# A linear-attention and expert kernel: the batch laid anew, with k projected early into another bank and v one batch ahead

## The reference, cut

```python
mod = (silu(c) @ wmod).reshape(16, 6, 1, 128)            # sa, ca, ga, sb, cb, gb for each batch
h = layernorm(x) * (1 + ca) + sa                         # x: 16 batches x 512 tokens x 128
# attention, 16 heads of 8, 32 random features:
q = (exp(qh @ orf.T / 8**0.25 - |qh|^2 / (2*sqrt(8))) + 1e-6) / sqrt(32)     # k the same way
kv = einsum('nlm,nld->nmd', k, v);  ksum = k.sum(1)
out = (q @ kv) / (q @ ksum)
x = x + ga * (out @ Wo.T + bo)
h = layernorm(x) * (1 + cb) + sb
e = argmax(h @ gate_W + gate_b)                          # one of 8 experts for each token
x = x + gb * (gelu(h @ W1[e] + b1[e]) @ W2[e] + b2[e])
```

## Time and profile before

| what | us |
|---|---|
| median of 3 runs | 383.06 |
| lowest and highest | 382.57, 385.99 |
| span of the profiled execution, first to last instruction | 360.6 |
| first phase in it, up to about | 212 |
| TensorE busy in the span | 338.8 (94%) |
| VectorE, ScalarE, GpSimd busy | 271.2, 265.1, 213.2 |

### The profile page before, as it was taken

How to read it: one execution, slowest core, us unless ns; L and a number is a source line. 1 busy time by engine, 2 the same in 40 slices (tenths; PEclk the granted TensorE clock), 3 DMA queues, 4 the chain that set the end, 5 groups by cost and what they waited for, 6 DMA issues and landing times.

```text
span 360.6 us, 13729 instructions
## 1 busy us (share of the span) xinstructions
PE 338.8 (94%) x4823; PEld 263.9 (73%) x4823; DVE 271.2 (75%) x1104; ACT 265.1 (74%) x644; POOL 213.2 (59%) x262
## 2 busy tenths in 40 slices
PE   6899999899988999998999999999999999999994
PEld 5445765566465566646665669999989999999993
DVE  3456997898879789878887978887677676666653
ACT  2688988799878888977888756676656667666761
POOL 3142386776667757857854618846767455545554
PEclk9999999999999999999999999999999999999999
DMA  7174656774566547444432467445657665545410
GB/s 233 50 253 166 210 184 221 259 243 160 177 227 205 176 167 230 163 132 156 153 133 100 149 163 227 142 118 150 194 161 269 209 184 147 147 128 135 137 38 12
DMA packets 40211, 60.47 MB, mean 168 GB/s; under 512 B 5426, under 2 KB 28086, under 8 KB 40016
## 3 DMA queue, kind: packets, MB, share of 16 engines
q1 hardware_dynamic: 33776, 42.54, 39.9%
q0 software_dynamic: 6368, 17.05, 12.5%
HBM read 28.63 MB, written 19.34 MB: 133 GB/s over the span
## 4 chain that ended last, share of the span: by engine, by line
PE 60%; ACT 15%; DMA 10%; DVE 6%; issue 5%; POOL 1%; SPq 1%; DVEq 1%; POOLq 0%; ACTq 0%
PE ps_proj L1350 16%; PE ps_feat L1337 9%; DMA qmix<-qsqs 9%; PE ps_proj L1132 6%; PE ps_den_gate L1337 4%; PE ps_proj L1182 4%; PE ps_kv L1337 4%; ACT qf L627 3%; ACT qvals L606 2%; ACT shared L588 2%; PE ps_kv L1198 2%; PE ps_out L1330 2%; ACT den L656 2%; ACT shared L581 2%; ACT kvm L600 2%
## 5 line engine op out<-in xcount | busy, mean ns | idle before, releaser
L545 POOL DMA_INDIRECT out<-kf,modb x71 | 70.1, 987 | 52.4 <-DVE kf L1060 47.0
L507 POOL DMA_INDIRECT experts_lists<-pay,slot x64 | 65.9, 1030 | 43.4 <-DVE slot L893 29.5
L1350 PE MATMUL ps_proj<-w2sb,qf 128*128 x568 | 75.0, 275 | 0.4 <-ACT qf L690 0.4
L1350 PEld LDWEIGHTS ps_proj<-w2sb,qf 128*128 128x128 f32 x568 | 68.9, 192 | 0.6 <-issue 0.6
L681 ACT ACTIVATE xT<-ps_out 128x128 f32<-128x128 f32 x71 | 19.7, 277 | 44.8 <-PE ps_out L1330 44.1
L1055 DVE TENSOR_TENSOR kf<-ps_proj,firsts_sb 128x128 f32<-128x128 f32 x71 | 20.7, 291 | 34.6 <-PE ps_proj L1350 22.6
L690 ACT ACTIVATE qf<-ps_feat,shared 128x128 f32<-128x128 f32 x144 | 40.9, 374 | 0.0
L1337 PE MATMUL ps_feat<-xT,shared 128*128 128x128 f32 x288 | 38.8, 277 | 1.5 <-issue 0.9
L1337 PEld LDWEIGHTS ps_feat<-xT,shared 128*128 128x128 f32 x288 | 35.0, 192 | 2.8 <-issue 1.7
L1132 PE MATMUL ps_proj<-shared,wsb 128*128 128x512 f32 x62 | 33.3, 620 | 1.0 <-ACT shared L581 0.4
L977 DVE COPY shared<-firsts_sb 128x516 f32 x71 | 31.4, 442 | 1.6 <-issue 1.5
(11 more groups left out here) (189 smaller groups left out, 890.3 us busy)
## 6 DMA issues: line engine op xcount, KB each, us to landing
modb<-experts_lists SPq DMA_DIRECT2D x71, 196.0 KB, 2.8
xall<-in_x SPq DMA_DIRECT2D x16, 256.0 KB, 3.0
pay<-modb SPq DMA_DIRECT2D x16, 256.0 KB, 3.0
qmix<-qvals SPq DMA_DIRECT2D x30, 128.0 KB
qmix<-qsqs SPq DMA_DIRECT2D x30, 128.0 KB
modb<-modulation_rows SPq DMA_DIRECT2D x4, 768.0 KB, 5.2
firsts_sb<-in_firsts SPq DMA_DIRECT2D x8, 322.0 KB, 4.2
w2sb<-in_w SPq DMA_DIRECT2D x8, 256.0 KB
```

Of the source, the lines that this page charges most:

```text
L507: g_.indirect_dma_start(out=lists, in_=pay[b.home][:, t, :], in_offset=None, out_offset=bass.IndirectOffsetOnAxis(ap=slot[b.home][:, t:t + ...
L545: g_.indirect_dma_start(out=rows_out, in_=yb[u], in_offset=None, out_offset=bass.IndirectOffsetOnAxis(ap=token, axis=0), bounds_check=last ...
L1350: ins = mm(Y[u % 2][:, 0:D], g[u % R4][:, c * P:(c + 1) * P], w2sb[:, bass.ds(e * DFF + c * D, D)], start=(c == 0), stop=(c == FC - 1))
```

## The change

No matmul, activation or DMA is added or removed; they are reordered, and three semaphores replace one.

- On TensorE `transpose_xn(b+1)` and the k projection of b+1 go right behind `k_features(b)` and `transpose_h2(b-2)`. The k projection writes G (`k_bank`), once `attention(b-1)` has read it. `q_features(b)` follows, then `out_project(b-1)`, the v projection of b+1 (before: that of b, ahead of the output product), `gate(b-2)`, `kv_product(b)`, the q projection of b+1, `kv_transpose(b)`, `gate_transpose(b-2)`, the constants and the denominator, `rank(b-2)`, the numerator.
- On ScalarE `modulate(b+1)` stands between the two `k_pair`s, `k_values` and `k_squares` of b+1 ahead of `q_pair(b, 0)`, `gateT` between the `q_pair`s; v's values, q's values and q's squares of b+1 follow `kvm_copy(b)`, ahead of `Ln` and `Exp`.
- On VectorE `centre_h2(b-1)` goes ahead of `kv_values(b)`; its half of `normalise1(b+2)` stands behind that; `experts(b-2)`, `eps_values`, `scale_h2` and then `slots(b-2)` follow.
- On GpSimd the first layer norm's roots go ahead of the second's.
- The first and the last batch have orders of their own.

The helpers' waits follow the new semaphores (`s_pk`, `s_pq`, `s_pv` for `s_proj`); that part, and the first batch's q features as a function of their own, are left out here.

```diff
@@ -335,6 +337,9 @@
         block = ctx.enter_context(nc.Block())
+        def k_bank(v):
+            return PJ[0] if v < 2 else G
+
...
@@ -469,6 +474,8 @@
                 if b is not None:
                     pool.wait_ge(s_xn1, b.v)
+                    if b.v > 2:
+                        pool.wait_ge(s_xna, b.v - 2)
...
@@ -514,10 +523,10 @@
                     pool.wait_ge(s_mb, 16)
                 if b.v >= EARLY_ROWS and (b.v - EARLY_ROWS) % LATE_ROWS == 0:
                     pool.wait_ge(s_mbl, 16 * ((b.v - EARLY_ROWS) // LATE_ROWS + 1))
+                if ahead and b.par == 0:
+                    rstd1_of(b.half + 3, b=b + 2)
                 if not first:
                     rstd2_of(b + -1, rows_of=None if second else b + -2)
-                if ahead and b.par == 0:
-                    rstd1_of(b.half + 3, b=b + 2)
                 if not first and not second:
                     scatter(b + -2, (0, 1))
...
@@ -634,30 +643,60 @@
                 act.wait_ge(s_lg, b.v + 1)
                 a.activation(lgT[:], I[:, 0:P], ACT.Copy).then_inc(s_lgT, 1)
-            def batch(b, first=False, second=False, last=False, ahead=True):
-                k_pair(b, 0)
-                if not first and not second:
-                    h2T_copy(b + -2)
-                k_pair(b, 1)
-                if not first and not second:
-                    gateT(b + -2)
-                v_values(b)
-                q_pair(b, 0, first)
-                if not last:
-                    modulate(b + 1)
-                q_pair(b, 1, first)
-                kvm_copy(b)
-                if not last:
-                    k_values(b + 1)
-                    k_squares(b + 1)
-                    q_values(b + 1)
+            def rden_first(b):
                 act.wait_ge(s_den, b.v + 1)
                 act.wait_ge(s_eps, b.v + 1)
                 a.activation(den[:], G[:], ACT.Ln, bias=kveps[:, 1:2]).then_inc(s_denp, 1)
                 act.wait_ge(s_denp, b.v + 1)
                 a.activation(rden[:], den[:], ACT.Exp, scale=-1.0).then_inc(s_rden, 1)
-                if not last:
-                    q_squares(b + 1)
+
+            def first_batch(b):
+                k_pair(b, 0)
+                k_pair(b, 1)
+                v_values(b)
+                q_pair(b, 0, first=True)
+                modulate(b + 1)
+                q_pair(b, 1, first=True)
+                k_values(b + 1)
+                k_squares(b + 1)
+                kvm_copy(b)
+                v_values(b + 1)
+                q_values(b + 1)
+                q_squares(b + 1)
+                rden_first(b)
+                normalise1(b + 2)
+
+            def last_batch(b):
+                k_pair(b, 0)
+                h2T_copy(b + -2)
+                k_pair(b, 1)
+                gateT(b + -2)
+                q_pair(b, 0)
+                q_pair(b, 1)
+                kvm_copy(b)
+                rden_first(b)
+
+            def batch(b, first=False, second=False, last=False, ahead=True):
+                if first:
+                    return first_batch(b)
+                if last:
+                    return last_batch(b)
+                k_pair(b, 0)
+                modulate(b + 1)
+                k_pair(b, 1)
+                if not second:
+                    h2T_copy(b + -2)
+                k_values(b + 1)
+                k_squares(b + 1)
+                q_pair(b, 0)
+                if not second:
+                    gateT(b + -2)
+                q_pair(b, 1)
+                kvm_copy(b)
+                v_values(b + 1)
+                q_values(b + 1)
+                q_squares(b + 1)
+                rden_first(b)
                 if b.v + 2 < B:
                     normalise1(b + 2)
...
@@ -729,6 +768,7 @@
             def centre_h2(b):
+                dve.wait_ge(s_var2, b.v + 1)
...
                                                  scalar=mv2[:, t, 0:1], in1=modb[:, b.v, CB, :],
@@ -776,8 +816,6 @@
                 dve.wait_ge(s_shift1, b.v + 1 if b.v < 2 else b.half + 2)
                 if b.v:
                     dve.wait_ge(s_t1, b.v)
-                if b.v >= 2:
-                    dve.wait_ge(s_xna, b.v - 1)
...
@@ -994,32 +1032,32 @@
                         first_moments(b.half + 2, marked=x_stats(b + 3, 1))
                     else:
                         x_stats(b + 3, 0)
-                if not first and not last:
-                    normalise1(b + 1, lo=LT // 2)
                 if not first:
                     residual(b + -1)
                     second_stats(b + -1)
+                if second:
+                    dve.wait_ge(s_mb, 16)
+                if b.v > EARLY_ROWS and (b.v - 1 - EARLY_ROWS) % LATE_ROWS == 0:
+                    dve.wait_ge(s_mbl, 16 * ((b.v - 1 - EARLY_ROWS) // LATE_ROWS + 1))
+                if not first and not last:
+                    centre_h2(b + -1)
                 if last:
                     table_rows(0)
-                    kv_values(b)
+                kv_values(b, first)
+                if last:
                     experts(b + -2)
                     dve.wait_ge(s_w1, 16 * E)
                     expert[0] = expert_of(0)
                     copy_firsts(0)
-                elif not first and not second:
+                if b.v + 2 < B:
+                    normalise1(b + 2, lo=LT // 2)
+                if not first and not second and not last:
                     experts(b + -2)
-                if not last:
-                    kv_values(b, first)
-                    if not first and not second:
-                        slots(b + -2)
-                if second:
-                    dve.wait_ge(s_mb, 16)
-                if b.v > EARLY_ROWS and (b.v - 1 - EARLY_ROWS) % LATE_ROWS == 0:
-                    dve.wait_ge(s_mbl, 16 * ((b.v - 1 - EARLY_ROWS) // LATE_ROWS + 1))
                 eps_values(b)
                 if not first and not last:
-                    centre_h2(b + -1)
                     scale_h2(b + -1)
+                if not first and not second and not last:
+                    slots(b + -2)
                 if b.v == B - 2:
                     early_counts()
                 if last:
...
@@ -1118,27 +1156,37 @@
             def transpose_xn(b):
                 pe.wait_ge(s_xn1, b.v + 1)
+                if b.v >= 2:
+                    pe.wait_ge(s_xna, b.v - 1)
                 if b.v:
                     pe.wait_ge(s_v, b.v)
                 for t in range(LT):
                     ins = tr(H[:, t * P:(t + 1) * P], xn1[:, t, :], ident)
                 ins.then_inc(s_t1, 1)
-            def project(b, i, first=False, bank=None):
+            def project_k(b):
                 pe.wait_ge(s_hT, b.v + 1)
-                if not first:
+                if b.v == 1:
+                    pe.wait_ge(s_exp, 2)
+                if b.v >= 2:
+                    pe.wait_ge(s_rdst, 2 * (b.v - 1))
+                mm(k_bank(b.v)[:, :], wsb[:, W_K:W_K + P], hT[:], start=True, stop=True).then_inc(s_pk, 1)
+
+            def project_q(b, bank=PJ[1]):
+
+                pe.wait_ge(s_hT, b.v + 1)
+                if b.v:
                     pe.wait_ge(s_exp, NC * b.v - 1)
-                mm((bank or PJ[i])[:, :], wsb[:, i * P:(i + 1) * P], hT[:], start=True, stop=True).then_inc(s_proj, 1)
-
-            def v_project(b, last=False):
-
-                if last:
-                    pe.wait_ge(s_end, 1)
+                mm(bank[:, :], wsb[:, W_Q:W_Q + P], hT[:], start=True, stop=True).then_inc(s_pq, 1)
+
+            def project_v(b):
+
+                pe.wait_ge(s_hT, b.v + 1)
                 for t in range(LT):
                     ins = mm(H[:, t * P:(t + 1) * P], hT[:, t * P:(t + 1) * P], wsb[:, W_V:W_V + D],
                              start=True, stop=True)
-                ins.then_inc(s_proj, 1)
+                ins.then_inc(s_pv, 1)
             def k_features(b, first=False):
...
@@ -1204,9 +1251,11 @@
                 pe.wait_ge(s_kvT, b.v + 1)
                 if first:
                     pe.wait_ge(s_exp, 3)
+                elif b.v < B - 1:
+                    pe.wait_ge(s_kst, 2 * b.v + 4)
                 tr(G[:, 0:P], kvT[:], ident).then_inc(s_kvt, 1)
-            def attend(b):
+            def eps_and_den(b):
                 pe.wait_ge(s_exp, NC * (b.v + 1))
                 pe.wait_ge(s_kvm, 2 * (b.v + 1))
                 kv = kvm[:, :, :, :, :].rearrange("p n c j i -> p n c (j i)")
@@ -1218,6 +1267,9 @@
                 for c in range(NC):
                     ins = mm(G[c * CW:(c + 1) * CW, :], kv[:, 1, c, :], qf[:, c, :], start=True, stop=True)
                 ins.then_inc(s_den, 1)
+
+            def numerator(b):
+                kv = kvm[:, :, :, :, :].rearrange("p n c j i -> p n c (j i)")
                 for c in range(NC):
                     ins = mm(KV[c * CW:(c + 1) * CW, :], kv[:, 0, c, :], qf[:, c, :], start=True, stop=True)
                 ins.then_inc(s_num, 1)
...
@@ -1275,40 +1327,62 @@
```

(82 more changed lines are left out.)

49 lines of the change are left out of this document (25 added, 24 removed).

## The result

The changed kernel takes **452.5 us** (median of 4 runs, 446.8 to 453.7) where the kernel before takes 384.5. The ratio is 1.1745, with an interval of 1.164 to 1.185; it is taken without the run of 453.7, the profiled one, which lies over 1.5% above the fastest. The forecast was 410 with a range of 401 to 417: the sign was right, the size was not. The profiled execution has a span of 451.9 us and a time of 453.7, so 1.8 us lie around the span.

The account below looks back on a forecast made before the run. TensorE, busy 94% of the span, bounds the kernel, which loses 0.65 us a batch at the qmix wait. Terms of 22.0 + 2.5 + 1.0 + 0.8 + 0.8 = 27.1 on 383.06 gave 410 us, range 401 to 417.

Parts of the forecast that it names:

- The path through a middle batch: Start-to-start steps of batches 2 to 14: next k features at 14.19 us, 22.0 us more in all.
- The stalls: TensorE's new waits in each batch: hT before the k projection 1.02 us, kvT about 0.6, kvm copy about 0.8.
- SyncE's queue: Rival, chance 0.07: `gate_rows` waits for a later-issued scatter, costs 1.5 us more than allowed, qmix stays late: 419.
- `count(0)`: At the start of the last batch it waits for batch 12's `slots`: 0.8 us.
- the tail: Batch 12's later scatters delay the first block's load by 0 to 1.7 us; 0.8 taken.
- tight, not late: `rank`'s one-hot rows, GpSimd's roots, G freed by `attention`: costed at nothing, a few tenths a batch if they slip.
- the pair starts when k features end, about 2.1: ScalarE's first `k_pair` starts about 2.1 us after k features start; its successor can start some 0.9 later.
- the 22 us around it stay: Time outside the profiled span of 360.6 us stays, so 383.06 + 27.1 gives 410.
- the case I gave 0.02: Rival, chance 0.02: new gaps let TensorE's clock fall to half speed; five such batches would be 59 us, 469.
- TensorE-only stalls (403): Rival, chance 0.24: VectorE's statistics and centring overlap better, kvT isn't late, period about 13.7 us: 403.
- no difference: Rival, chance 0.03: half the stall at hT is hidden, VectorE isn't late, gain and loss cancel: 383.
- faster: Rival, chance 0.04: the stalls don't appear and every batch takes 11.85 us: 375.

Follow-up runs that it names:

- e13: The changed kernel, unchanged, run again on a chip where the kernel before takes 362.4 us: 394.3 us, ratio 1.0875.
- e6: The changed kernel with GpSimd's scatters moved behind the gated rows, on the slower kind of chip: 408.9 us.
- e5: The kernel before, unchanged, profiled on the slower kind of chip: 379.1 us.
- e14: The changed kernel with GpSimd's scatters moved behind the gated rows, again, on the faster kind of chip: 395.1 us, ratio 1.093.
- e1: The changed kernel with `rank` moved from between denominator and numerator to behind the next batch's k features: 443.7 us.
- e3: The changed kernel with 14 small filler matmuls between the transposes of xn and the k projection: 439.5 us.
- e4: The kernel before with q's squares put ahead of the denominator's logarithm and exponential: 389.0 us against 385.0, ratio 1.012.
- e2: The kernel before with `rank` moved from behind `gate_transpose` to between denominator and numerator: 407.1 us.
- e8: The changed kernel with VectorE's copy of the kv product put ahead of the centring of h2: 449.7 us.
- e9: The changed kernel with scatters behind the gated rows and the kv copy ahead of the centring of h2, on the faster kind of chip: 394.2 us.
- e18: The changed kernel with one scatter instead of two ahead of the gated rows, on the faster kind of chip: 396.4 us.
- e7: The kernel before with GpSimd's scatters moved behind the gated rows: 406.2 us against 384.5, ratio 1.056.

## Why the prediction was right and wrong

**The path through a middle batch was right on kind B.** Batch 8 of e13, timeline of TensorE, then of VectorE, k features at 126.98 (they start again at 141.35):

```profile
129.47 0.60 PE L1164 MATMUL ps_out<-csb,shared 128*128 128x128 f32 x4
130.93 1.13 PE L1174 MATMUL ps_den_gate<-shared,wsb 128*128 128x512 f32 x2 [0.87 <-ACT shared L590]
131.99 0.66 PE L1229 MATMUL ps_proj<-qmix,feat_q 32*64 32x512 f32 x4
133.03 1.16 PE L1283 MATMUL ps_kv<-wo,oT 128*128 128x128 f32 x8
...
137.93 0.33 PE L1256 MATMUL ps_den_gate<-csb,kvT 128*128 128x128 f32 x1 [0.52 <-DVE kvT L854]
139.01 0.27 PE L1264 MATMUL ps_feat<-kf,kvm 128*32 128x1 f32 x13 [0.64 <-ACT kvm L609]
```

```profile
134.23 0.69 DVE L883 TENSOR_TENSOR pay<-xall,ps_kv 128x512 f32<-128x512 f32 x1 [2.88 <-PE ps_kv L1283]
135.86 0.38 DVE L894 BATCH_NORM_AGGREGATE mv<-st 128x2 f32<-128x6 f32 x4
136.34 1.14 DVE L773 SCALAR_TENSOR_TENSOR pay<-pay,mv,modb 128x128 f32<-128x128 f32 x4
137.40 0.48 DVE L854 SCALAR_TENSOR_TENSOR kvT<-ps_kv,csb 128x64 f32<-128x64 f32 x2
```

| step, us from k features | forecast | e13 |
|---|---|---|
| `transpose_xn` | 2.49 | 2.49 |
| k projection | 4.01 | 3.95 |
| `q_features` | 5.06 | 5.01 |
| `out_project` | 6.11 | 6.05 |
| variances of h2 | 8.85 | 8.88 |
| `kv_values` | 10.47 | 10.42 |
| `kv_transpose` | 11.01 | 10.95 |
| constants | 12.09 | 12.03 |
| next k features | 14.19 | 14.37 |

The stalls: hT 1.02 forecast, 0.87 here and 0.94 in the mean (13.1 us, 14 times); kvT 0.6, 0.52; kvm 0.8, 0.64. No wait on qmix is in the list, so SyncE's queue did no harm.

**On kind B the sum of the order was 27.1, measured 30.7** (spans, 391.3 less 360.6): batch 0 0.95 (forecast 1.0), batch 1 2.6 (2.5), batches 2 to 14 with `count(0)` 25.6 (22.8), the tail 1.8 (0.8), the second phase -0.4 (0), and 0.1 ahead of batch 0. The mis-sized term is the middle batches. Undisturbed ones take 14.3, not 14.2: their last step, from the constants to the next k features, was put at 1.98 + 0.12 = 2.10 and takes 2.34. The other 1.4 us are spread, mostly over k features that end 0.2 us late in batches 3, 4 and 12, a k projection 0.25 us late in 7, one-hot rows that come 0.25 us late for `rank` in 4, the one of the three "tight, not late" steps that shows. `count(0)` was right: batch 15 starts 15.02 us into batch 14, forecast 14.19 + 0.8.

**The step that failed: "the pair starts when k features end, about 2.1".** On kind A, where the result was measured, the first exponential starts 4.1 to 4.4 us behind k features in every batch from 3 on. The change also puts `modulate` right behind that exponential, so hT and the k projection follow it: the projection starts 5.84 us into batch 3 and 5.86 into batch 4, forecast 4.01. What makes it late is the scatters (e6). The prediction had worked out that they begin about 0.6 us behind k features instead of 1.06 ahead of them, and priced this for the first block's load alone; it put at nothing what they do to the matmuls beside them.

The cost: on kind A the changed kernel's last k features start 42.8 us later than on kind B (271.0 and 228.2). At full clock, in batches 3 and 4, a period is 1.5 us longer than in e13 (16.18 and 16.20 against 14.53 and 14.79); 12 of them are some 18 us. The rest, some 24 us, fits the clock: the dips of the first phase last 47.8 us, in which a TensorE that is busy throughout does 23.9 us of work less. The second phase is 17.8 us longer, of which the kernel before shows 13.8 as well (e5). e6 confirms it from the other side: moving the scatters alone gives 44 us back and leaves 408.9, near the 410 that the forecast gives without the late k features. The agreement is part luck: there the kernel before is delayed by its own scatters too (e5), and with late scatters the order costs 24 us on kind A and 33 on kind B (e14).

**A premise that was wrong as well: "the 22 us around it stay".** Every profiled execution that has a time has 1.8 or 1.9 us around its span. The other 20 us or so are inside the kernel as it runs on kind A; the profile was of kind B. This did not make the 42 us of the miss: 27.1 was added to a median of kind A, where the result was measured too. What it cost is the warning. The profile that every step was read from showed k features of 2.1 us, and on kind A, where the kernel had been timed, they take 2.3 to 3.2 (e5). On kind B the forecast would have been 360.6 + 1.8 + 27.1 = 389.5, against 394.3 measured.

The upper bound is wider than the reason given for it: 13 batches at 0.4 us are 5, so 415, not 417. It changes nothing here.

**The rivals.** The clock did fall, the case I gave 0.02 and ruled out because the granted clock had stood through all waits of the kernel before. That argument was from 11.85 us of matmuls in 12.5. The changed batches had TensorE busy for 13.44 of 16.20 us in the batch ahead of the first dip (70.6 to 86.8), and it then stood idle for 3.06 us until 92.95; e1's were busy for 12.55 of 16.00; in e13 it is busy for 12.27 of 14.30 (batch 8) and the first phase has no dip. By the Trainium skill ("TensorE: Matmul & The Clock Gate", the part on PSUM-queue cycling) frequent short idles can make the clock swing. The trace agrees in part: the clock does swing where the waits of TensorE have grown, and filling one of them cut the time at half speed to a third (e3), but in e6 on kind A and e13 on kind B, with the same TensorE order and gaps of up to 0.9 and 1.2 us, it stays at full speed through the first phase. So the three gaps of the forecast alone were not enough. TensorE-only stalls (403) falls by the table: kvT was late by what VectorE's chain said. SyncE's queue, no difference and faster fall with the waits.

**What stays open.** That the place of the scatters decides whether k features are late on kind A is shown (e6 with `rank` in place, e4 and e2 beside it). Through what is not. In batches 3, 4, 6, 8, 12 and 14 TensorE's own matmuls start late, as shown above. In batches 5, 7, 10, 11 and 13 they start as on kind B, and the h2 transposes at 2.00 us, and yet the exponential comes after 4.1 to 4.4 us. Batch 5 of the changed kernel, k features from 86.80, TensorE and ScalarE:

```profile
88.80 0.66 PE L1291 MATMUL ps_den_gate<-csb,pay 128*128 128x128 f32 x4
91.20 1.02 ACT L629 ACTIVATE kf<-ps_feat 128x1024 f32<-128x1024 f32 x1 [3.02 <-remote]
92.95 1.22 PE L1174 MATMUL ps_den_gate<-shared,wsb 128*128 128x512 f32 x1 [3.06 <-ACT shared L590]
```

So it is either the end of the matmuls, which the profile only models, or the signal of it that comes late; the engines wait for nothing that the profile names ("issue", "remote"). The transfers of batch 3 keep the DMA engines as busy on either kind (0.54 of 16.2 us, 0.58 of 14.5). Nor is it known why a chip is of one kind or the other. e1 to e8 ran on two chips, both of kind A, and then e9 to e18 on two others, both of kind B, one of them in two sittings. No chip was seen as both kinds, and the execution shown ahead of the prediction, earlier than all of them, is taken to be of kind B. So it is likely the chip and not the hour, but it isn't shown.

## What to carry to other kernels

Before a forecast is added to a median, the profile's span must be set against that median: a gap of 6% may be another chip, not overhead, and the same order can cost 32 us on one chip and 68 on another. A reordering moves everything that hangs on it: here VectorE's `slots` set when GpSimd's scatters start, and some 2.3 us of that moved the first of them from ahead of k features (-1.4 us) into them (+0.9). Price the covers between neighbours by start-to-start distances, as it worked here to 0.1 us on one kind of chip, then ask where the DMAs issued behind each moved step now fall, and what reads the result of the matmuls beside them.

## What the runs showed of the hardware

- The kernel before takes 384 us on some chips and 363 on others; 14 of the 17 us between two spans lie in the second phase, where single blocks take up to 4.6 us (e5) instead of the 1.9 of most.
- With scatters issued 0.9 to 1.35 us into k features, the exponential that reads them starts after 4.1 to 4.4 us instead of 2.1 on the slower kind of chip. On the other it starts after 2.1 us in most batches and 2.5 at most (e13).
- With scatters behind the gated rows in the kernel before, ScalarE's copy of the gate's product starts up to 2.9 us behind it instead of 0.49 on the slower kind (e7).
- A cast of 4 elements per partition on VectorE takes 1.22 us instead of 0.17 while GpSimd adds into `xall`, in five batches of e14. The transposes of h2 on TensorE wait for it and start 2.5 us into the batch instead of 2.0, and the next batch follows after 14.8 us instead of 14.3; `attention`, behind the cast on VectorE, starts 2.28 us into the batch instead of 0.91. VectorE, then GpSimd, both in e14:

```profile
113.35 1.22 DVE L929 CAST slot<-slot_f 128x4 int32<-128x4 f32 x1
```

```profile
113.28 1.26 POOL L510 TENSOR_TENSOR xall<-xall,bog 128x512 f32<-128x512 f32 x1
```

  The Trainium skill ("SBUF — State Buffer", the part on who interferes with whom) says that a cast on VectorE in a two-port mode and a GpSimd instruction share one pair of ports, and that the one which comes second waits for the whole of the first. The trace agrees, with 0.07 us between the starts and 0.03 between the ends; in which mode the cast ran, it doesn't show.
